# A graph network's node sums: two fp32 products a tile, or six bf16 products with the rows split into exact parts

## The reference

```
h = sage_layer(h, ...)                       # three layers; the third has 64 outputs
    # relu(h @ w_self + (segment_sum(h[src], dst) / deg) @ w_neigh + b)
x = layernorm(x + h)
# gcn_conv, twice, the first with relu behind it
    # norm[:, None] * (x @ W)[src], segment_sum over dst, + b
x = layernorm(x + gcn(x))
```

## Time and profile before

| | us |
|---|---|
| median of 3 executions | 5115.66 (5112.63 to 5118.18) |
| span of the profiled execution | 5104.4 |
| third layer, about | 1640 to 2235 |
| first convolution, about | 2235 to 2790 |
| TensorE matmul busy | 4188.4 (82%) |
| VectorE busy | 3326.6 (65%) |
| GpSimd busy | 3288.9 (64%) |
| ScalarE busy | 2761.8 (54%) |

### The profile page before, as it was taken

One profiled execution on the slowest core, in us unless ns is written; L12 is line 12 of the kernel. 1 busy time (PEld: TensorE's weight loads), 2 busy tenths in 40 slices (PEclk: granted clock), 3 DMA queues, 4 the chain that ended last, 5 costly groups with the idle time before them and its releaser, 6 DMA issues. The chain is left out here.

```text
span 5104.4 us, 115936 instructions
## 1 busy us (share of the span) xinstructions
PE 4188.4 (82%) x31393; PEld 3787.4 (74%) x31394; DVE 3326.6 (65%) x6783; ACT 2761.8 (54%) x7100; POOL 3288.9 (64%) x3162
## 2 busy tenths in 40 slices
PE   2999999799997899979997455548878599999997
PEld 1899999799997898879997454536667366666666
DVE  5555555677775788857676666758888355555555
ACT  0566666455554778754443566656666244444444
POOL 2544443578773777747775777747775677777772
PEclk9999999899999999989999767779999799999999
DMA  1677777466665678758876566657776244444442
GB/s 35 213 252 252 253 251 245 173 233 241 232 235 209 223 258 264 258 198 276 280 265 222 163 186 186 186 148 214 219 210 201 73 121 117 116 117 118 117 115 90
DMA packets 490326, 991.05 MB, mean 194 GB/s; under 512 B 156821, under 2 KB 246965, under 8 KB 470968
## 3 DMA queue, kind: packets, MB, share of 16 engines
q1 hardware_dynamic: 389368, 872.44, 50.6%
q0 software_dynamic: 100800, 116.72, 10.9%
HBM read 452.18 MB, written 380.15 MB: 163 GB/s over the span
## 5 line engine op out<-in xcount | busy, mean ns | idle before, releaser
L749 PE MATMUL ps_all<-arena 128*128 x16000 | 2028.0, 286 | 500.5 <-DMA arena<-arena 365.3
L749 PEld LDWEIGHTS ps_all<-arena 128*128 128x128 f32 x16000 | 1993.3, 204 | 549.1 <-issue 544.7
L678 POOL DMA_INDIRECT arena<-n_t,ix_now x784 | 905.1, 1154 | 429.5 <-issue 404.7
L678 POOL DMA_INDIRECT arena<-y_t,ix_now x784 | 808.3, 1031 | 349.8 <-issue 331.9
L1128 ACT ACTIVATE arena<-bytes 128x2048 f32<-128x2048 uint8 (+1 forms) x300 | 475.9, 1618 | 299.6 <-DMA bytes<-pairs_d 209.2
L678 POOL DMA_INDIRECT arena<-x_rows,ix_now x392 | 373.1, 952 | 375.4 <-PE ps_all L749 263.4
L1639 PE MATMUL ps_all<-w,tp 128*128 128x128 f32 x4000 | 490.9, 276 | 28.8 <-ACT store_b L1782 28.2
L1639 PEld LDWEIGHTS ps_all<-w,tp 128*128 128x128 f32 x4000 | 477.9, 192 | 47.2 <-issue 38.6
L678 POOL DMA_INDIRECT arena<-x_t,ix_now x392 | 385.9, 985 | 191.4 <-issue 172.0
L708 DVE TENSOR_TENSOR arena<-iota,window 128x1024 f32<-128x1024 f32 x302 | 363.4, 1219 | 100.8 <-ACT bytes L1093 93.9
L1093 ACT ACTIVATE bytes<-arena 128x1024 uint8<-128x1024 f32 (+1 forms) x200 | 296.7, 1484 | 241.7 <-DMA pairs_d<-bytes 235.2
(11 more groups left out here) (204 smaller groups left out, 7653.8 us busy)
## 6 DMA issues: line engine op xcount, KB each, us to landing
x_t<-store_a SPq DMA_DIRECT2D x150, 512.0 KB, 3.1
s_t<-store_a SPq DMA_DIRECT2D x50, 1024.0 KB
n_t<-store_b SPq DMA_DIRECT2D x50, 1024.0 KB
load_a<-s_t SPq DMA_DIRECT2D x50, 1024.0 KB
bytes<-pairs_d SPq DMA_DIRECT2D x100, 512.0 KB
y_t<-store_b SPq DMA_DIRECT2D x100, 512.0 KB, 2.9
load_b<-x_t SPq DMA_DIRECT2D x100, 512.0 KB
arena<-arena SPq DMA_DIRECT2D x147, 192.0 KB
```

What stands on the lines that cost most here:

```text
L678: pool.indirect_dma_start(out=slot_rows(at, W, pitch), out_offset=None, in_=table, in_offset=bass.IndirectOffsetOnAxis(ap=ix_now[:, at:at ...
L749: last = pe.matmul(out(j, 2) if wide else out(j, 1), hot, both(rows) if wide else rows, start=(k == 0), stop=(k == n - 1))
```

## The change

In the third layer and the first convolution a slot becomes three times as wide. VectorE splits each gathered fp32 number r into three that add up to it: the upper half of r's bits (a bf16), the upper half of what is left, and the rest; it writes the two remainders as fp32 beside the row (`split`), and TensorE reads only the upper halves, with a step of two. The one-hots are widened to bf16 instead of fp32. A tile of nodes is then six bf16 matmuls of 64 columns (two windows by three parts) in place of two fp32 matmuls. TensorE waits for the semaphore `parts`, which VectorE's second subtraction signals, where it waited for the gathers. VectorE splits block m+3 between the outputs of m and the centring of m+1 in the third layer, and block m+2 behind the take of m+1 in the first convolution.

```
+    def part_of(slot, k):
+        return arena.bitcast(BF16)[:, bass.ds(slot * (6 * D), 6 * D)].rearrange("p (k w o) -> p k w o", k=3, o=2)[:, k, :, 1]
+
+    def sums_of_parts(pe, tiles, bank, at, places):
+        first = tiles[0]
+        for j in tiles:
+            out = bank[:, (j % GT) * D:(j % GT + 1) * D]
+            for w in range(2):
+                for k in range(3):
+                    last = pe.matmul(out, bf16_hots(at, j // GT)[:, w, j % GT, :], part_of(places[w][j - first], k),
+                                     start=(w + k == 0), stop=(w + k == 3))
         return last
...
         def rows_in(self, pe, m, i, u):
             if not has_edges(m):
                 return
-            if self.two_windows:
+            if self.in_parts:
+                pe.wait_ge(S("parts"), now(m))
+            elif self.two_windows:
                 pe.wait_ge(S(f"rows{u}"), landed(f"rows{u}", i, ET))
...
+            if self.in_parts:
+                sums_of_parts(pe, range(q * GT, q * GT + GT), self.bank(u, q), self.hot_at(u), places).then_inc(S(f"agg{q}"), 1)
+                return
...
+        def split(self, ve, m, i, u, windows):
+            if not windows or not has_edges(m):
+                return
+            ve.wait_ge(S(f"rows{u}"), landed(f"rows{u}", i, ET))
+            at = (m % RB) * (ET * 3 * D)
+            slots3 = arena[:, bass.ds(at, ET * 3 * D)].rearrange("p (t k w) -> p t k w", t=ET, k=3)
+            tops = arena.bitcast(BF16)[:, bass.ds(at * 2, ET * 6 * D)].rearrange("p (t k w o) -> p t k w o", t=ET, k=3, o=2)[:, :, :, :, 1]
+            nc.vector.tensor_tensor(slots3[:, :, 1, :], slots3[:, :, 0, :], tops[:, :, 0, :], ALU.subtract).then_inc(S("rest"), 1)
+            ve.wait_ge(S("rest"), now(m))
+            nc.vector.tensor_tensor(slots3[:, :, 2, :], slots3[:, :, 1, :], tops[:, :, 1, :], ALU.subtract).then_inc(S("parts"), 1)
...
-            nc.scalar.activation(hot_matrices(self.hot_at(u), q, self.two_windows), kept_matrices(u, q, self.two_windows),
-                                 ACT.Copy).then_inc(S(f"hot{q}"), 1)
+            hots = bf16_hots(self.hot_at(u), q) if self.in_parts else hot_matrices(self.hot_at(u), q, self.two_windows)
+            nc.scalar.activation(hots, kept_matrices(u, q, self.two_windows), ACT.Copy).then_inc(S(f"hot{q}"), 1)
...
     class Sage2(Pass):
+        in_parts = True
+        pitch = 3 * D
...
         def vector(self, ve, m, i, u, windows):
             V = nc.vector
             self.stored(ve, i, u)
             norm_out(ve, m, store_a[u])
+            self.split(ve, m + 3, i + 1 + u, 1 - u, windows)
             self.center(ve, m + 1)
...
     class Gcn1(Pass):
+        in_parts = True
+        pitch = 3 * D
...
         def vector(self, ve, m, i, u, windows):
             V = nc.vector
             self.take_block(ve, *later(m, i, u), windows)
-            self.hots_ahead(ve, m, u, windows)
+            self.split(ve, m + 2, i + 1, u, windows)
```

More of the change, by code:

```diff
@@ L657, in slot_rows @@
     def slot_rows(s, W, pitch):
-        return ring[:, s * pitch:s * pitch + W]
+        return arena[:, s * pitch:s * pitch + W]
     LEAD = 3
@@ L750, in sums, with bf16_hots @@
                                  both(rows) if wide else rows, start=(k == 0), stop=(k == n - 1))
+        return last
+    def bf16_hots(at, q):
+        return arena[:, at:at + HOT].bitcast(BF16).rearrange("p (q k j n) -> p q k j n", q=2, k=2, j=GT)[:, q]
+    def part_of(slot, k):
[8 more added lines that the diff above has]
+                                     start=(w + k == 0), stop=(w + k == 3))
         return last
@@ L1003, in build @@
         two_windows = False
+        in_parts = False
         skew_lead = 2
@@ L1063, in collect @@
             self.bank_free(pe, m, q)
+            if self.in_parts:
+                sums_of_parts(pe, range(q * GT, q * GT + GT), self.bank(u, q), self.hot_at(u), places).then_inc(S(f"agg{q}"), 1)
+                return
             sums(pe, range(q * GT, q * GT + GT), lambda j, n: self.bank(u, q)[:, (j % GT) * D:(j % GT + n) * D],
                  D, self.hot_at(u), places).then_inc(S(f"agg{q}"), 1)
+        def split(self, ve, m, i, u, windows):
[8 more added lines that the diff above has]
+            nc.vector.tensor_tensor(slots3[:, :, 2, :], slots3[:, :, 1, :], tops[:, :, 1, :], ALU.subtract).then_inc(S("parts"), 1)
         def hot_at(self, u):
+            if self.in_parts:
+                return RING * self.pitch + u * HOT
             if self.two_windows:
@@ L1296, in vector_loop @@
         def vector_loop(self, ve, windows):
+            for m in range(3):
+                self.split(ve, m, m // 2, m % 2, windows)
             self.gather_in(ve, 0, 0, 0, windows)
@@ L1299, in vector_loop @@
             self.gather_in(ve, 1, 0, 1, windows)
-            bodies(ve, lambda m, i, u: self.vector(ve, m, i, u, windows), by=TURN if windows else 2)
+            bodies(ve, lambda m, i, u: self.vector(ve, m, i, u, windows), by=TURN if windows else 2, behind=4)
         def vector(self, ve, m, i, u, windows):
@@ L1406, in vector_loop @@
             self.residue(ve, 0, 0, 0)
-            super().vector_loop(ve, windows)
+            for m in range(2):
+                self.split(ve, m, 0, m, windows)
+            self.take_block(ve, 0, 0, 0, windows)
+            bodies(ve, lambda m, i, u: self.vector(ve, m, i, u, windows), by=TURN if windows else 2, behind=4)
         def vector(self, ve, m, i, u, windows):
```

## The result

The changed kernel takes 5850.97 us, the median of four executions (5838.57 to 5853.53), against 5116.39 for the kernel before on the same chip: a ratio of 1.143, 95% interval 1.141 to 1.145. It is 735 us slower, 76 us more than forecast. The profiled execution has a span of 5836.8 us.

The account below looks back on a forecast made before the run. The prediction took TensorE's sequencer, issuing address instructions, to become the bound: 16.1 us a block in the third layer, 17.9 in the first convolution. Over 50 blocks 252 + 367, plus 40 for the clock, made 5775 us, range 5460 to 5980.

Parts of the forecast that it names:

- The array drops out of the sum: Node sums: a bf16 pass costs TensorE's array between 0.03 and 0.112 us, under the sequencer's step of 0.125.
- 96 steps of 0.125 us: Node sums: TensorE's sequencer issues 96 address instructions a block where 32 were, 12.0 us a block.
- Loads, waits and branch: Rest of the sequencer's block: register loads 3.0 us, waits and static instructions 0.95, the loop's branch 0.15.
- The clock: Both passes: a lower granted clock slows products and transposes, 0.4 us a block, +40 us; bounds 0 and 2.8 a block.
- The stall in the first convolution: TensorE's collection of m+2 waits for VectorE's split after a 3.5 us chain: 1.8 us a block, bounds zero and 3.5.
- The split in the third layer: VectorE has the parts after 6 us, TensorE wants them after about 8.5: no stall, 2 us to spare.
- Sum: Both passes: 252 + 367 + 40 = 659 us more on the profiled span, a forecast time of 5775 us.
- the cheaper sequencer (1): Both passes: the sequencer binds at a step of 0.105 us with the stall hidden, 5455 us; chance 0.13.
- the array (2): Both passes: the array binds at half clock, 0.16 us a pass, about +1015 us, 6130 us; chance 0.08.
- The other side (3): Both passes: address steps and passes so short that VectorE binds and the change wins, 5000 us; chance 0.06.

Follow-up runs that it names:

- a_two: The changed kernel with two bf16 matmuls a tile and window where three stood, so 64 addresses a block: 5471.5 us, ratio 1.071.
- a_splitfirst2: The changed kernel with VectorE splitting block m+2 before it takes up block m+1 in the first convolution: 5821.1 us, ratio 1.139.
- a_halfprod: The kernel of a_splitfirst2 with half of the fp32 product matmuls left out: 16.96 and 17.18 us a block, 6850 us in all on a slower chip.
- e_static2: The changed kernel with all bf16 node-sum matmuls reading one fixed place, so without address instructions: 5104.7 us, ratio 1.000.
- b_addresses3: The kernel before with three address instructions of 7 operations before each node-sum matmul where one of 3 stood: 25.96 and 25.69 us a block, 7684 us, slower chip.
- a_wide: The changed kernel with bf16 matmuls of 128 data columns instead of 64, each row read twice: 17.81 and 18.57 us a block, 6931 us, slower chip.
- b_split: The kernel before with wider slots, VectorE's split and TensorE's wait for it, node sums still fp32 matmuls: 5205.0 us, ratio 1.018.
- a_splitfirst: The same kernel as a_splitfirst2, run on a slower chip: 18.28 us a block in the first convolution, 6924 us in all.

## Why the prediction was right, and where it was off

The mechanism held: the limit moved from the array to TensorE's sequencer, and the periods are sums of what it issues. The trace allows the whole sum to be taken. Here each row of the sequencer counts from its start to the start of the next, over forty blocks:

| us a block | addresses | register loads | waits | other | period |
|---|---|---|---|---|---|
| forecast, third layer | 12.0, and 0.4 for the clock | 3.0 | 1.1 with other | | 16.5 |
| forecast, first convolution | 12.0, and 0.4 for the clock | 3.0 | 2.9 with other | | 18.3 |
| changed, third layer | 13.61 | 2.70 | 0.70 | 0.71 | 17.73 |
| changed, first convolution | 12.74 | 3.14 | 2.27 | 0.66 | 18.82 |
| a_two, third layer | 9.42 | 3.53 | 0.70 | 0.71 | 14.37 |
| a_splitfirst2, first convolution | 13.52 | 3.38 | 0.70 | 0.67 | 18.27 |
| a_halfprod, third layer | 12.74 | 2.80 | 0.70 | 0.72 | 16.96 |
| a_halfprod, first convolution | 12.74 | 3.08 | 0.70 | 0.66 | 17.18 |

The register loads of the changed kernel in 36 blocks of the third layer and of the first convolution:

```profile
L730 PEldq TENSOR_LOAD <-slots x144: 587/590/957, 1857.1 to 2487.4; - x144
```

```profile
L730 PEldq TENSOR_LOAD <-slots x144: 586/591/1567, 2762.2 to 3431.7; - x144
```

Step by step:

1. *The array drops out of the sum.* Right. The bounds of 0.03 and 0.112 us a pass hold what e_static2 measured, 0.030 from start to start (0.053 at the lower level). The formula of the Trainium skill, "TensorE: Matmul & The Clock Gate", section "LDWEIGHTS (loading the stationary operand)", has 107 ns for each of these weight loads, by which the changed sums lose on the array too; the same page says that full-width weight loads of other types than fp32 can be faster, which the prediction left out. The passes, load and matmul together, came 30 ns apart, so the formula does not hold for them.
2. *96 steps of 0.125 us, bounds 0.105 and 0.127.* Mis-sized: 0.133 with free room in the queue, above my upper bound. Of every three addresses one is 60 ns long, with four operations instead of three, and has 0.138 to the next, and a few steps of a collection are 0.15 to 0.17. I had priced all by the rows of before, where each is 46 ns long. That is 96 x 0.008 = 0.8 us a block, +77 us: as much as the whole miss, though other terms miss too and cancel.
3. *Loads, waits and branch, 4.1 us.* Right in the third layer (4.11). In the first convolution 4.50 without the stall: I took 0.59 us, the least of rows 12, for every register load, whose median there is 0.67; measured are 0.61 on average in the third layer and 0.72 in the first convolution, with single ones of 1.57. What makes them longer is not shown.
4. *The clock, 0.4 us a block in both passes.* Its size was near and its way another. What it costs is the queue that fills behind the products, 0.77 us a block in the third layer by a_halfprod (0.87 in the address steps alone), and nothing in the first convolution, where the wait gives the array its time.
5. *The stall in the first convolution, 1.8 us.* The chain came link by link, 3.4 of 3.5 us; the stall was 1.57. It does not add to point 4, as I had it: taking the wait away gave 0.55 us back, not 1.57. On the kernel before, with short sequencer work, the same chain costs 1.92.
6. *The split in the third layer: no stall, 2 us to spare.* Right, 2.4 us.
7. *Sum.* Forecast per block 16.5 and 18.3 with the clock, measured 17.73 and 18.82: +61 and +25 us of the miss; 13 come back elsewhere, and the median stands 14.2 us above the profiled span where I took 11.3. By the table, over 50 blocks: +74 us from the steps (point 2, both passes), +23 and -20 from the clock (point 4, third layer and first convolution), +20 from the register loads (point 3), -11 from the stall (point 5), -13 and +3 as said: 76. That the first convolution came within 25 us is partly luck, since errors of both signs cancelled there.

Of the rivals, the cheaper sequencer (1) and the array (2) are out. The other side (3) was rightly unlikely, but its price was wrong, and so was the thought that a cheaper matmul was worth having here at all: at a step of 0.03 us I had 10.45 and 8.7 us a block, -31 and -85 us, a time of 5000; measured without addresses are 10.78 and 10.91, no gain. VectorE and, in the first convolution, the gathers on which the split waits, stand right behind TensorE's 11.07 and 10.57. GpSimd's 316.8 busy microseconds of 423 and the transfers' share of 0.81 should have warned me.

No version here beats the kernel before. Two things stay open: which of gathers, transfers and the split's place sets the 10.9 us of the first convolution without addresses, and what lengthens the register loads. No run keeps the three parts of a row with correct sums and fewer addresses.

## What to carry to other kernels

Count what an engine's sequencer has to issue before counting what its array has to do: a matmul on an address from a register costs the sequencer at least 0.12 us here, so cutting one 0.224 us product into three cheap ones triples the part that can't be made cheap. Read the distance of address instructions in a place where the queue has room, and count the operations in each; then ask which other engine has its period within a few per cent, before calling the full engine's time worth saving. A wait and a full queue in the same block are not simply added: here the wait of 1.57 us hid 0.8 us of full queue. And don't take a wait, or a load, from one block: the block shown had 1.3 us of stall where forty had 1.57 on average.

## What the runs showed of the hardware

- An address instruction is 46, 60, 138 and 158 ns long with three, four, six and seven register operations. With two or four matmul instructions between, the next one starts 78 ns after its end at the least (after, before, b_addresses3); with none between, 58 (b_addresses3).
- A bf16 matmul with 128x128 weights and 64 columns that needs no address follows the last after 30 ns at full clock and 53 at the lower level (e_static2); its row shows 96 ns for the weight load alone. The duration of such a row is no price.
- The mean granted clock of the third layer rose from 0.64 to 0.81, and its period went from 17.73 to 17.81 us a block (a_wide, on a slower chip).
- A register load from the table takes 0.59 us at the least; the means of the two passes run from 0.61 to 1.04 us (changed kernel and b_split, both in the third layer), and single loads reach 2.1.
- The same program took 5821 us on one chip and 6924 on another, with granted clocks of 0.64 and 0.64 in the third layer and 0.65 and 0.66 in the first convolution. The last pass, from about 4620 and 5020 us on, moved the same data at these rates:

```profile
DMA packets 85943, 134.21 MB, mean 114 GB/s; under 512 B 36608, under 2 KB 46752, under 8 KB 85909
```

```profile
DMA packets 85945, 134.18 MB, mean 71 GB/s; under 512 B 36625, under 2 KB 46769, under 8 KB 85911
```

(The kernel of a_splitfirst2, then a_splitfirst.) Passes bounded by a sequencer did not change by 1%.
